# One core, attention beside a mixture of experts: a reordered front loop, and two attention blocks written out over their batches with the seam between them overlapped

## The reference

```
xn = layernorm(x)
# branch s, per batch of 2048 tokens, 16 heads of 16
Q, K, V = ln(xn@Wq+bq), ln(xn@Wk+bk), ln(xn@Wv+bv)
phiQ, phiK = tanh(Q@Wphi_q+b)+1, tanh(K@Wphi_k+b)+1
alpha = softmax over tokens of (mean of Q over tokens . K / 4) * 2048
KV, K_sum = sums over tokens of phiK*alpha (x V)
attn = (phiQ @ KV) / (phiQ @ K_sum);  attn += 0.1 * (grouped conv over 5 tokens + b)
attn = ln(attn);  s = attn + gelu(attn@W1+b1)@W2+b2 + xn       # hidden width 1024
# branch g: the axis of 4 batches is the sequence, 2048 rows stand beside it
ln1 = ln(xn); q (16 heads), k, v (4 heads) = ln1 @ Wqkv.T      # width 384
after = xn + causal_attention(q, k, v over 4 positions) @ Wproj.T
ln2 = ln(after); probs = softmax(ln2 @ Wr.T) over 16 experts; top 2
buf[expert, slot] = ln2 (up to 1280 slots); h2 = gelu(buf@W1[e])@W2[e]
g = after + sum over 2 of h2[expert, slot] * prob
return x + s * silu(g)
```

## Time and profile before

| | |
|---|---|
| median of 3 runs | 2302.94 us (2302.5 to 2305.48) |
| the profiled execution | 2310.01 us, its span 2308.2 us |
| mean granted PE clock | 0.912 of full speed |
| busy over the span | PE 82%, PEld 72%, DVE 65%, POOL 40%, ACT 36% |
| front loop | from 58 to about 494 us |
| routing | 494 to about 510 us |
| attend(0), batches 0 and 1 | 520 to 808, 816 to 1101 us |
| MoE | 1107 to 1605 us |
| attend(2), batches 2 and 3 | 1612 to 1959, 1969 to 2304 us |

### The profile page before, as it was taken

One profiled execution on the slowest core, in us unless ns is written; L12 is line 12 of the kernel. 1 busy time (PEld: TensorE's weight loads), 2 busy tenths in 40 slices (PEclk: granted clock), 3 DMA queues, 4 the chain that ended last, 5 costly groups with the idle time before them and its releaser, 6 DMA issues. The chain is left out here.

```text
span 2308.2 us, 43949 instructions
## 1 busy us (share of the span) xinstructions
PE 1897.7 (82%) x12647; PEld 1664.1 (72%) x12648; DVE 1493.7 (65%) x3800; ACT 829.9 (36%) x1976; POOL 930.1 (40%) x1404
## 2 busy tenths in 40 slices
PE   1777777638899878998799999999678897578888
PEld 1455555426689865898799999999455887465887
DVE  3688787744455443565588787776574677564677
ACT  2455444415433244232233333333352332352322
POOL 4344344305545355453323333220560554560553
PEclk7788888869999989999899999999788999798999
DMA  4323322111211112111344443342441122341112
GB/s 146 114 101 125 126 100 100 49 47 53 81 59 58 40 55 74 62 51 40 119 124 124 120 122 109 118 122 73 127 122 44 40 63 70 112 119 42 46 57 70
DMA packets 154822, 197.44 MB, mean 86 GB/s; under 512 B 19913, under 2 KB 140047, under 8 KB 152542
## 3 DMA queue, kind: packets, MB, share of 16 engines
q1 hardware_dynamic: 111598, 124.26, 17.6%
q0 software_dynamic: 16928, 49.43, 7.0%
q10 hardware_dynamic: 26064, 20.99, 2.7%
HBM read 107.34 MB, written 88.21 MB: 85 GB/s over the span
## 5 line engine op out<-in xcount | busy, mean ns | idle before, releaser
L1667 ACT ACTIVATE hid<-bank 128x512 f32<-128x512 f32 x160 | 95.8, 598 | 331.1 <-PE bank L128 326.7
L126 PE MATMUL bank<-rows_hi,up_hi 128*128 128x256 f32 x640 | 188.4, 294 | 6.1 <-POOL up_lo L1733 6.1
L128 PE MATMUL bank<-rows_hi,up_lo 128*128 128x256 f32 x640 | 181.8, 284 | 0.0
L127 PE MATMUL bank<-rows_lo,up_hi 128*128 128x256 f32 x640 | 181.7, 284 | 0.0
L128 PE MATMUL bank<-down_hi,hid_lo 128*128 128x256 f32 x640 | 181.2, 283 | 0.0
L126 PE MATMUL bank<-down_hi,hid_hi 128*128 128x256 f32 x640 | 181.1, 283 | 0.0
L127 PE MATMUL bank<-down_lo,hid_hi 128*128 128x256 f32 x640 | 181.1, 283 | 0.0
L1770 DVE TENSOR_TENSOR hid_lo<-hid,hid_hi 128x512 fp32r<-128x512 f32 x160 | 140.8, 895 | 55.1 <-ACT hid_hi L1667 53.9
L1085 POOL DMA_INDIRECT job_picked<-h_d,where x128 | 134.6, 1051 | 92.2 <-issue 24.4
L1082 POOL DMA_INDIRECT buf_d<-lt,where x128 | 131.8, 1030 | 93.1 <-issue 70.7
L1370 PE MATMUL bank<-wconv,knt 128*128 128x128 f32 x1280 | 156.3, 278 | 0.0
(11 more groups left out here) (301 smaller groups left out, 5819.6 us busy)
## 6 DMA issues: line engine op xcount, KB each, us to landing
buf_d<-zeros SPq DMA_DIRECT2D x16, 1280.0 KB, 7.7
rows_in<-buf_d SPq DMA_DIRECT2D x80, 256.0 KB, 3.1
h_d<-h ACTq DMA_DIRECT2D x80, 256.0 KB, 3.5
xa<-in_x SPq DMA_DIRECT2D x20, 512.0 KB, 5.1
x<-in_x SPq DMA_DIRECT2D x16, 512.0 KB, 5.1
after_d<-after SPq DMA_DIRECT2D x16, 512.0 KB, 3.0
ln_d<-ln SPq DMA_DIRECT2D x16, 512.0 KB, 3.3
lt<-ln_d SPq DMA_DIRECT2D x64, 128.0 KB
```

Of the source, the lines that this page charges most:

```text
L126: pe.matmul(dst, hi, mhi, start=start and i == 0, stop=False)
L127: pe.matmul(dst, hi, mlo, start=False, stop=False)
L128: mm = pe.matmul(dst, lo, mhi, start=False, stop=end)
L1667: act.activation(dst[:, 2 * half:2 * half + 2].rearrange("p f c -> p (f c)"), bank[half][:], ACT.Gelu_apprx_tanh).then_inc(e_hid, 1)
```

## The change

**Front loop.** The bias of qkv is gone as a matmul: the constant part is folded into the weights and a bias of 1 on xn1. `att` is no longer added up by DVE: PE adds the ten weighed products while it turns them (20 plain matmuls with the identity as weights, adding in PSUM) in place of 8 transposes. The pick leaves the loop: ACT copies the logits of each turn, and the routing block finds both experts of all 64 tiles at once, in ten more steps on DVE over 1024 elements and some small ones. The copies of qkv are shared out, two tiles to ACT and two to DVE. The parts stand in another order on PE, ACT and DVE; the transposes of ln2 use banks 0 and 1.

**Both attention blocks.** The hardware loop over two batches is gone; `flow` calls written-out functions. The next batch's first four steps of statistics and norms are issued in steps 14 to 17 of the second loop, and its first loop's steps 0 to 3 beside steps 18 to 21. Banks of the first loop and the place of `xtile` are moved so that both can be live. All waits are for constants, `hold` and the copy of the row numbers (`where`) are gone there, and the picks of a batch start three steps later (`LATE`). The MoE is not touched.

```
@@ setup
+                        step(dve.scalar_tensor_tensor(wqkv[:, j], bank[0][:, 0:QKV], 1.0 / E, wqkv[:, j], ALU.mult, ALU.add))
@@ front loop, scalar
-                                act.activation(xn1[:, s], xn[t.odd][:, s], ACT.Copy,
+                                act.activation(xn1[:, s], xn[t.odd][:, s], ACT.Identity, bias=one_col[:, 0:1],
                                                scale=norm[t.odd][:, 2, s:s + 1]).then_inc(xn1_made, 1)
...
-                            act.wait_ge(router_step, t.n * ROUTE + 3)
-                            act.activation(rprob[:], logit[:], ACT.Exp).then_inc(rexp_done, 1)
+                            act.wait_ge(router_done, t.n + 1)
+                            act.activation(logits[:, :, bass.ds(t.n, 1), :].rearrange("p s b n -> p (s b) n"),
+                                           bank[4][:].rearrange("p (s n) -> p s n", s=S)[:, :, 0:NX], ACT.Copy).then_inc(logit_made, 1)
@@ front loop, tensor
-                            pe.wait_ge(mha_step, t.n * MHA + MHA)
...
-                            turned(att[t.odd], bank[2:4], att_turned)
+                            pe.wait_ge(weighed_made, t.n * 7 + 7)
+                            for j in range(HALVES):
+                                for i, (s, u) in enumerate(PAIRS):
+                                    part = early[t.odd][:, i] if i < 3 else weighed[:, i - 3]
+                                    last = pe.matmul(bank[2 + j][:, s * P:(s + 1) * P], part[:, j * P:(j + 1) * P], ident[:],
+                                                     start=u == 0, stop=u == s)
+                                last.then_inc(att_turned, 1)
...
-                                pe.matmul(bank[4 + s % 2][:, 0:QKV], one_rows[:], brow2[:, ROW_QKV:], start=True, stop=False)
                                 for j in range(HALVES):
-                                    mm = pe.matmul(bank[4 + s % 2][:, 0:QKV], xnt[:, j, s * P:(s + 1) * P], wqkv[:, j],
-                                                   start=False, stop=j == 1)
+                                    mm = pe.matmul(bank[5 - s % 2][:, 0:QKV], xnt[:, j, s * P:(s + 1) * P], wqkv[:, j],
+                                                   start=j == 0, stop=j == 1)
@@ front loop, vector
-                        step(dve.tensor_tensor(att[t.odd][:, 1], prod[:, 1], prod[:, 2], ALU.add))
...
-                        step(dve.tensor_reduce(att[t.odd][:, 2], weighed[:, 0:3].rearrange("p u c -> p c u"), AX_X, ALU.add))
...
-                        step(dve.tensor_reduce(att[t.odd][:, 3], weighed[:, 3:7].rearrange("p u c -> p c u"), AX_X, ALU.add))
...
+                            keep_qkv(t0.back(1), 3)
...
+                            keep_qkv(t0, 1)
@@ routing, vector
+                    step(dve.tensor_tensor(logit, logit, router_bias[:].unsqueeze(1).to_broadcast((P, TILES, NX)), ALU.add))
+                    step(dve.tensor_reduce(highest[:], logit, AX_X, ALU.max))
+                    step(dve.tensor_tensor(logit, logit, over(highest[:]), ALU.subtract))
+                    step(dve.scalar_tensor_tensor(ranked[:], logit, 0.0, ranks, ALU.is_equal, ALU.mult))
+                    step(dve.tensor_reduce(rank[:, :, 0], ranked[:], AX_X, ALU.max))
+                    step(dve.tensor_tensor(hot[0][:], ranks, over(rank[:, :, 0]), ALU.is_equal))
+                    step(dve.scalar_tensor_tensor(place[:], hot[0][:], -1e30, logit, ALU.mult, ALU.add))
+                    step(dve.tensor_reduce(second[:], place[:], AX_X, ALU.max))
+                    step(dve.tensor_tensor(ranked[:], place[:], over(second[:]), ALU.is_equal))
+                    step(dve.tensor_tensor(ranked[:], ranked[:], ranks, ALU.mult))
+                    step(dve.tensor_reduce(rank[:, :, 1], ranked[:], AX_X, ALU.max))
+                    step(dve.tensor_tensor(hot[1][:], ranks, over(rank[:, :, 1]), ALU.is_equal))
...
@@ attend
+        OPEN, LAG, FIRST_STEPS, SECOND_STEPS, LATE = 14, 18, BT + 5, BT + 6, 3
+        X_BANK, QK_BANKS, V_BANKS, TURN_BANK, PHIK_BANK = 2, (6, 4), (5, 3), 7, 0
...
+                def down_bank(n):
+                    return bank[n % 2 if n >= BT - 2 else (7, 3)[n % 2]]
+
+                def flow(opening, first_loop, middle, second_loop):
+                    for b in batches:
+                        if b == first:
+                            for i in range(OPEN, LAG):
+                                opening(b, i)
+                            for i in range(FIRST_STEPS):
+                                first_loop(b, i)
+                        else:
+                            for i in range(SECOND_STEPS - LAG, FIRST_STEPS):
+                                first_loop(b, i)
+                        middle(b)
+                        for i in range(SECOND_STEPS):
+                            second_loop(b, i)
+                            if b == first and OPEN <= i < LAG:
+                                opening(b + 1, i)
+                            if b == first and i >= LAG:
+                                first_loop(b + 1, i - LAG)
...
-                        with pool.Fori(0, 2) as h:
-                            b = h + first
...
-                                    hold(pool, aq_mv, b * (3 * BT) + 3 * k + 3, pool_passed)
...
-                                    hold(dve, c_stats, b * BT + k + 1, dve_passed)
+                                dve.wait_ge(c_stats, b * BT + k + 1)
```

More of the change, by code:

```diff
@@ L393, in build @@
             weighed = sb("weighed", [P, 7, E], F32, own)
-            att = [sb(f"att{p}", [P, S, E], F32, own) for p in range(2)]
+            early = [sb(f"early{p}", [P, 3, E], F32, own) for p in range(2)]
             score = sb("score", [P, S, H, S], F32, own)
@@ L910, in attend @@
                 sout = [mine(f"sout{p}", [P, E]) for p in range(2)]
[L911 removed]
+                xtile = [[w[:, p].rearrange("p (j c) -> p j c", j=HALVES) for w in ant_s[0]] for p in range(2)]
                 if scatters:
@@ new lines, in attend, with job_of, own, is_own @@
+                amid = range(BT // 2, EACH - BT + 4) if scatters else ()
+                def job_of(b, j):
+                    return (b - first) * EACH + j
+                def own(b, n):
+                    return job_of(b, BT + n)
+                def is_own(job):
+                    return job % EACH >= BT
+                def batch_tile(job):
+                    b, j = batches[job // EACH], job % EACH
+                    return b * BT + j - BT if is_own(job) else (b - 2) * BT + j
+                def rounds(job):
+                    return job // ring + 1
```

1251 lines of the change are left out of this document (625 added, 626 removed).

## The result

The changed kernel takes 2144.36 us (2138.27 to 2148.51, 4 runs) against 2302.72 for the kernel before: a ratio of 0.930 (95% interval 0.9279 to 0.9321). The forecast was 2157 us, 13 above. The profiled execution took 2144.18 us with a span of 2142.5, so 165.7 us of span are gone. Against the sum of the prediction, 2164 for the profiled execution, that is 20 us less; the median misses its forecast by 13 only because the profiled execution before ran 7 us above its median and the one after did not.

What follows compares the result with a forecast made beforehand. No engine full in the front loop, PE and DVE waiting in turn; PE bounds attend(0), attend(2) looser. 2310.0 - 55 + 13 - 46 - 60 + 2 = 2164 profiled, times 0.9969 is 2157 us; range 2110 to 2215.

Steps and rivals of the forecast that it cites:

- Front: Front loop: 2.8 us less in each of 16 turns (45) and 10 at the last three turns, -55 us.
- together 21.6, 21.8 with the lower clock: Front turn: 18.5 us PE work, waits of 1.3 and 1.8, 0.2 for lower clock; 21.8 us, from 24.6.
- The credit for the bias matmuls: Front loop on PE: dropping four bias matmuls gives back 4 x 0.5 = 2.0 us a turn.
- rival B: Front loop clock stays at 0.81, turn 24.7 us, 47 us less gain: 2204 us; chance 0.12.
- rival E: Front loop slower: additions come in a burst, loop settles at 1.2 GHz, up to 2431 us; chance 0.04.
- C: Overlap of batches doesn't pay: only 10 of 50 us come, 2197 us; chance 0.08.
- seams: Changes of batch: overlap fills PE's idle time and low clock, 22 us in attend(0) and 28 in attend(2).
- D: More than priced: front turn 20.5 us (-21), holds count in full (-16), 2120 us; chance 0.14.
- the holds: Extra semaphore instructions on POOL and DVE in the attention blocks gone: 24 us in attend(0), 19 + 13 in attend(2).
- picks three steps late: Attend(2): picks that begin three steps later cost 0, bounds -5 to +10 us.
- What else: Remaining terms: table loads for tanh +2 us, MoE unchanged, longer written-out code 0.
- Table loads: ACT's tanh table load, 1.28 us at each batch's start, four times, now half hidden: +2 us, bounds 0 to +5.

Runs made afterwards that it cites:

- bias_back: Changed kernel with a matmul of biases put before each of the four qkv products in the front loop, output the same: 2155.74 us.
- no_overlap: Changed kernel, but a batch's opening and first steps are issued only behind the end of the batch before, on every engine: 2174.53 us.
- holds_back: Changed kernel with the extra semaphore instruction put back behind the waits of POOL and DVE in both attention blocks, overlap kept: 2193.28 us.
- no_overlap_late0: As no_overlap, with the first-loop picks in the third and fourth batch begun at step 0 instead of 3: 2165.23 us.
- all_undone: Changed kernel without batch overlap, picks from step 0, extra semaphore instructions back on POOL, DVE and SP, code still written out: 2204.49 us.
- front_only: New front loop and routing block of the changed kernel with both old attention blocks: 2254.25 us.
- best: Changed kernel with DVE making three xn1 tiles, early expert finding, third batch's picks at step 0, ACT writing alternate high parts, ln2 reordered: 2088.06 us.

## Why the prediction was right, point by point

**Front, -55 against -64.5.** The step "together 21.6, 21.8 with the lower clock" gave the turn, and it came to 21.3. Its parts held: 18.5 us of PE work, and 0.2 for the lower clock behind the waits, against 18.8 for both (the copy of xn took 1.98 for 1.8), and waits of 1.3 and 1.8 against 1.57 and 1.12. Undersized were the turns, 45 against 50 (3.35 in each of 15), and the end of the loop, -10 against -13.6 (from the last transposes of xn1 to the first step of the routing 64.9 us before, 51.3 after). The credit for the bias matmuls was wrong as a step, 2.0 us a turn against 0.5 (bias_back), but it stood only in the comparison with the old work and not in the sum of the new turn, so it did not reach the forecast.

**The clock and the rivals.** The mean in the front rose from 0.81 to 0.95, so rival B (the clock stays) and rival E (1.2 GHz throughout) fall. C (the overlap doesn't pay) let only 10 of the seams' 50 us come; 30 came, halfway between it and the forecast. D (more than priced) had the holds in full and a front turn of 20.5; neither came (46 us for the holds, where even the forecast had 56, and 21.3), though the total lies between D's 2120 and the forecast. By the rule in the Trainium skill (TensorE: Matmul & The Clock Gate, "Part 4: PE-mode transpose") that the prediction names, fewer transposes should lift the clock, and the sign agrees: 0.81 with 24 transposes a turn, 0.95 with 16. But the waits shrank in the same change, and no run separates the two.

**Routing, +13 against +12.1.** Ten steps of 1.22 in a chain, as priced.

**Attend(0), -46 against -38; attend(2), -60 against -75.5.** The sum of both, -106 against -113.5, is nearer than its terms. Taken apart by the runs:

| term | forecast | measured |
|---|---|---|
| seams | 22 + 28 | 15.5 + 14.5 (no_overlap) |
| extra semaphore instructions | 24 + 32 | 15.4 + 30.3 (holds_back) |
| picks three steps late | 0 | -7, a loss (no_overlap_late0) |
| all else in the old loop: registers, row numbers, SP's order, banks, the wait at a batch's end | 0 | 12.7 + 39.3 (all_undone against front_only) |

The measured terms give 43.6 and 77.1 us, against the 38.0 and 75.5 of the two traces. The first three, taken out one by one, give 30.9 and 37.8, and all three together 26.5 and 30.0 (all_undone against the changed kernel); that is hardly more than two traces of the same code differ by.

So two steps failed, and their errors had opposite signs. One is the reading of the earlier trace rows: I put all of PE's idle time and low clock at the change of batch down to the drain, where no_overlap shows that only 30 of the 50 us come back with it. The other is the step "What else", which named nothing more that hangs on the old loop and so put it all at nothing. That left out the largest single cost in attend(2), 39 us, of which the addresses in registers are the part that the trace lets one see. It was to be seen before: the gap of 0.21 us before L1426 has no `hold` in front of it. That seams too large and this cost at nothing cancelled, so that the sum of both blocks came to within 8 us, was luck.

**Table loads, +2.** No run prices this term, and the traces show no cost in it. The changed kernel makes 9 loads of 1283 ns where before made 10. The prediction placed the loads for tanh inside the first loop; three of them stand in the middle instead, before the softmax, where ACT then waits for DVE anyway:

```profile
823.60 1.28 ACT L1238 ACT_TABLE_LOAD   x1
832.85 0.68 ACT L1238 ACTIVATE xa<-bank,small 16x512 f32<-16x512 f32 x1 [7.97 <-DVE small L1568]
```

The load at the second batch's start in the kernel before was followed by idle time on ACT too (2.88 us). One for the hidden layer, which both kernels have, shows how a load stands on ACT when nothing hides it:

```profile
605.49 0.39 ACT L1275 ACTIVATE ant_hi<-bank 128x256 fp32r<-128x256 f32 x1 [1.09 <-PE bank L1433]
605.89 1.28 ACT L1288 ACT_TABLE_LOAD   x1
607.19 0.84 ACT L1288 ACTIVATE tk<-bank,b1c 128x256 f32<-128x256 f32 x2
```

It begins when the activation before it ends and costs 1.3 us in all. By the 2.66 us that the Trainium skill (ScalarE: Activation LUTs, "What ACT_TABLE_LOAD costs") gives for a switch with its drain, a further 1.4 us should stand here; in this trace it doesn't.

**Longer code, 0.** Held: 2.19 MB of instructions in place of 2.76.

## What to carry to other kernels

Before a hardware loop of two turns is kept for its short code, count what hangs on its variable. Each wait with an added semaphore instruction showed here as 0.1 us on POOL (0.4 for two before a pick), and each address from a register as 0.2 on DVE. All that went with the loop's form, the extra instructions (49 us) and the rest that was not taken apart (50), was worth more than the overlap of batches that writing the loop out allowed (30). When idle time at a seam is priced, compare it with what the same code costs without the overlap, not with an ideal of full work. A row's start is no price either: a matmul's row can begin while the one before it still runs, so measure from the start of one product to the start of the next. And in a loop in which engines wait for one another in turn, take the waits one at a time from the bound engine's rows, and expect part of each back: half of xn1 moved to DVE gave 0.8 us a turn of a wait of 1.57, and the third tile with the order of ln2 gave 1.0 of two waits of 1.8 together.

## What the runs showed of the hardware that I had not expected

- A float32 product with 384 columns (two matmuls, four records) takes 1.29 us from start to start, with or without a bias matmul before it; the bias matmul, of float32r and one record, adds 0.17 us although its row is 0.63 long (changed and bias_back).
- A semaphore instruction behind a wait costs 0.10 us between two small steps on POOL (0.18 against 0.08), but 0.40 for the pair in front of an indirect DMA (0.90 against 0.50) (holds_back against changed).
- An operand whose address hangs on a register puts 0.21 us before the instruction on DVE (L1426 of before); with a fixed address it is 0.03, also where the wait's value is in a register (L1428 of before, L1483 of all_undone).
- DVE scales and shifts a tile of 128x256 from SBUF to SBUF in 0.3 us (0.88 for three, best), ACT in 0.52 (2.07 for four, changed).
